# Embedding gathers spread over the first items' loop, the row table filled in a small and a large pass, and both norms of the first layer taken from one set of statistics

## The reference, cut to what matters

```python
h = jnp.take(W.T, x, axis=0)          # x: (16, 256) ids below 12564; W: (256, 50257) -> 4096 rows of 256 floats
t = _layernorm(h)                      # no gain, no shift
for l in range(6):                     # "attention" over the 16 sequences
    n = layernorm(t, gamma[l], beta[l])
    q, k, v = split(n @ w_qkv[l]); q = softmax(q, axis=1); k = softmax(k, axis=2)
    ctx = einsum('bic,bjc->bij', k, v)
    t = einsum('bic,bij->bjc', q, ctx) @ w_out[l] + b_out[l] + t
h = h + t
# then top-2 of 8 experts (SwiGLU) and a shared expert on layernorm(h), added to h
```

## Time and profile before

| what | value |
|---|---|
| median of 3 runs | 1470.19 us (1468.88 to 1470.64) |
| the profiled execution's own time | 1476.68 us |
| its span, first to last instruction | 1474.9 us |
| mean granted TensorE clock | 0.946 |
| PE / DVE / ACT / POOL busy | 87% / 71% / 56% / 65% of the span |
| DMA traffic | 157.13 MB, mean 107 GB/s |

### The profile page before, as it was taken

The page is one execution under the profiler, slowest core; times in us unless marked ns, Lnnn a source line. Parts: engine busy times, 40 slices in busy tenths (PEclk is TensorE's granted clock), DMA queues, the critical chain, the costliest instruction groups (busy, mean ns, idle before and its releaser), DMA issues. The chain is left out here.

```text
span 1474.9 us, 37041 instructions
## 1 busy us (share of the span) xinstructions
PE 1277.8 (87%) x10992; PEld 1053.6 (71%) x10993; DVE 1043.0 (71%) x2675; ACT 831.4 (56%) x2286; POOL 960.0 (65%) x958
## 2 busy tenths in 40 slices
PE   4400499999999999999999999879989999999996
PEld 3400388888888888888888888645557888788884
DVE  3245789998998899899889999756564444444442
ACT  1230388778778877787787777765632322222221
POOL 0057789889889888988898889558640333333333
PEclk8755799999999999999999999979999999999998
DMA  9993264543463355346332546554433434444440
GB/s 320 380 319 118 47 127 102 138 87 69 102 133 64 64 131 108 64 89 142 70 65 58 116 87 107 97 84 127 128 125 102 67 54 58 70 57 58 63 60 8
DMA packets 354415, 157.13 MB, mean 107 GB/s; under 512 B 283953, under 2 KB 338737, under 8 KB 354353
## 3 DMA queue, kind: packets, MB, share of 16 engines
q1 hardware_dynamic: 321090, 117.99, 35.8%
q0 software_dynamic: 20064, 25.32, 9.3%
q10 hardware_dynamic: 13200, 13.11, 2.5%
HBM read 44.50 MB, written 42.64 MB: 59 GB/s over the span
## 5 line engine op out<-in xcount | busy, mean ns | idle before, releaser
L731 PE MATMUL bank<-hT,Wc 128*128 128x256 f16 x2304 | 285.8, 274 | 88.0 <-DMA hT<-hhl 76.0
L731 PEld LDWEIGHTS bank<-hT,Wc 128*128 128x128 f16 x2304 | 226.7, 98 | 115.9 <-issue 88.5
L691 POOL DMA_INDIRECT out_rows<-h0b,payin x78 | 121.5, 1557 | 235.4 <-DVE h0b L1471 182.8
L828 PE MATMUL bank<-xTg,Wall 128*128 128x256 f16 x1872 | 211.1, 273 | 0.0
L828 PEld LDWEIGHTS bank<-xTg,Wall 128*128 x1872 | 183.2, 98 | 21.4
L1096 ACT ACTIVATE silu<-bank 128x512 f32<-128x512 f32 x110 | 65.6, 596 | 215.0 <-PE bank L828 177.0
L596 POOL TENSOR_TENSOR h0b<-h0b,rows 128x512 f32<-128x512 f32 x96 | 121.9, 1269 | 98.0 <-issue 52.6
L1399 DVE SCALAR_TENSOR_TENSOR gT<-bank,silu 128x512 f32<-128x512 f32 x110 | 76.0, 691 | 130.2 <-ACT silu L1096 124.3
L731 PE MATMUL bank<-Wc,MT 128*128 128x256 f16 x1152 | 143.3, 275 | 9.8 <-DVE MT L1262 9.8
L731 PE MATMUL bank<-khl,eqT 128*128 128x256 f16 x1152 | 142.4, 274 | 6.0 <-DVE khl L1274 0.3
L731 PE MATMUL bank<-Wc,hT 128*128 128x256 f16 x1152 | 142.0, 273 | 0.0
(11 more groups left out here) (150 smaller groups left out, 2585.8 us busy)
## 6 DMA issues: line engine op xcount, KB each, us to landing
Wall<-in_L_tok_W SPq DMA_DIRECT2D x25, 512.0 KB, 7.8
emb_rows<-Wall ACTq DMA_DIRECT2D x25, 512.0 KB, 11.7
Wall<-in_L_ffn_ew SPq DMA_DIRECT2D x24, 512.0 KB
Wc<-Wn SPq DMA_DIRECT2D x48, 128.0 KB
Wst<-in_L_attn_w_qkv SPq DMA_DIRECT2D x12, 384.0 KB
h_rows<-Wall SPq DMA_DIRECT2D x4, 1024.0 KB, 4.4
X<-h_rows POOLq DMA_DIRECT2D x8, 512.0 KB, 6.6
out_rows<-X SPq DMA_DIRECT2D x8, 512.0 KB
```

Source lines behind the costliest of these rows:

```text
L691: pool.indirect_dma_start(out=out_rows, out_offset=bass.IndirectOffsetOnAxis(ap=got(j % PAYS, w, 0, i32), axis=0), in_=yout[j % 2][:, w, : ...
L731: last = mm(to, lhs(a, k, o), moving, start=(i == 0 and k == 0), stop=(i == 2 and k == 1))
L828: last = mm(to, cols(a, e, 2 * k + w, (2 * half + c) * P, P), moving, start=(n_ == 0), stop=(n_ == 5))
```

## The change

It has five parts.
1. The table is split in two DRAM tensors. `emb_near` has 2560 rows (one step) and is filled and gathered from in a loop of passes; `emb_last` has 10240 rows (`VLAST` = 4 steps) and is filled once. With these ids there is one pass, then the four steps. A gather from either tensor skips the rows whose index is out of its bounds. A block of 512 rows of `emb_last` is first filled with zeros (`s_fill`).
2. POOL issues 32 gathers from `emb_near` as soon as the first step has landed, then moves the indices on by 2560 (an index that was already served is moved out of reach). The gathers from `emb_last` are issued item by item, two for each: items 0 and 1 ahead of the loop, item t+7 inside iteration t.
3. For layer 0 there are no `first_stats`, `first_root` and `first_norm`. The statistics are taken of `G`; if v is the variance, POOL computes the inverse roots of v+eps and of v(1+eps)+eps^2, and the two norms follow from these. DVE in `norm` makes two small products (`eratio`), the doubly normed row, and from it X with b_out added, which POOL did before. For items 0 to 15 ACT makes the high half of h (`hhl`) and POOL the fp32 form and the low half.
4. The first layer's weights are loaded ahead of steps 2 to 5 of the table, split between the chunks of step 2, and installed before the table's end. The first twelve iterations are written out (`HEAD`), and the splitting of layer 1's weights runs in iterations 3 to 10.
5. `G` is stored to `h0_rows` in eight pieces inside the loop. The experts' slices are converted in layers 1 to 3, one in every iteration, so the first eight iterations of each of these layers have both a CUT and a slice.

```diff
-            n = stretches(pool)
+            n = passes(pool)
             with pool.Fori(0, n) as q:
                 for j in range(VBUF):
-                    pool.wait_ge(s_wst[j], (q + 1) * (STRETCH * 16))
+                    pool.wait_ge(s_wst[j], (q + 2) * 16)
                 pool.sem_inc(s_passed, 1)
+                for t in range(NT):
+                    gather(t, emb_near, s_gath[t % 4])
                 for g in range(4):
-                    gather(g)
-                for g in range(4):
-                    pool.wait_ge(s_gath[g], (q + 1) * 128)
+                    pool.wait_ge(s_gath[g], (q + 1) * (16 * NT // 4))
                 pool.sem_inc(s_passed, 1)
-
-                pool.tensor_scalar(idx[:, :], idx[:, :], -VROWS, None, ALU.add).then_inc(s_reuse, 1)
+                pool.tensor_scalar(far[:, :], idx[:, :], VSTEP, FAR, ALU.is_lt, ALU.mult).then_inc(s_far, 1)
+                pool.wait_ge(s_far, q * 2 + 1)
+                pool.sem_inc(s_passed, 1)
+                pool.tensor_tensor(idx[:, :], idx[:, :], far[:, :], ALU.add).then_inc(s_far, 1)
+                pool.wait_ge(s_far, q * 2 + 2)
+                pool.sem_inc(s_passed, 1)
+                pool.tensor_scalar(idx[:, :], idx[:, :], -VSTEP, None, ALU.add).then_inc(s_reuse, 1)
...
+            for j in range(VBUF):
+                pool.wait_ge(s_wst[j], (n + VLAST + 1) * 16)
+            pool.sem_inc(s_passed, 1)
+
+            def gather_item(i):
+
+                if i >= 4:
+                    pool.wait_ge(s_item[i % 4], 16 * TB * (i // 4))
+                for t in range(TB * i, TB * (i + 1)):
+                    gather(t, emb_last, s_item[i % 4])
...
+                if early(t + 4) and t >= 0:
+                    pool.wait_ge(s_hh, t + 5)
+                    low_half(t + 4, p)
+                if early(u):
+                    pool.wait_ge(s_rows, 48)
+                    pool.wait_ge(s_xb, u + 1)
+                    pool.tensor_tensor(xn[:, :, :], xn[:, :, :], row(0), ALU.mult).then_inc(s_hg, 1)
+                    pool.wait_ge(s_hg, u + 1)
+                    if u >= 1:
+                        pool.wait_ge(s_h, u)
+                    pool.tensor_tensor(hf[:, :, :], xn[:, :, :], row(1), ALU.add).then_inc(s_hf, 1)
+                    if t + 7 < NB:
+                        gather_item(t + 7)
+                    if t < -1:
+                        pool.wait_ge(s_hh, u + 1)
+                        low_half(u, 1 - p)
...
+                if early(w):
+                    pool.wait_ge(s_amv, w + 1)
+                    if w >= 2:
+                        pool.wait_ge(s_xb, w - 1)
+                    pool.tensor_scalar(evar[p][:, TB:], amv[p][:, :, 1], EPS, None, ALU.add)
+                    pool.tensor_scalar(evar[p][:, 0:TB], amv[p][:, :, 1], 1.0 + EPS, EPS * EPS, ALU.mult, ALU.add).then_inc(s_avar, 1)
+                    pool.wait_ge(s_avar, w + 1)
+                    pool.tensor_tensor(erstd[p][:, :], evar[p][:, :], mhalf[:, 0:2 * TB], ALU.pow).then_inc(s_arstd, 1)
...
+            act.dma_start(emb_last[VROWS - 2 * VCH:VROWS - VCH, :].rearrange("(v p) d -> p v d", p=P), h0b[:, 0, :, :]).then_inc(s_fill, 16)
...
+                    chunk(step, j, emb_last, VROWS - VCH if f_ == VLAST - 1 and j == VBUF - 1 else r0)
+                    if f_ == 0:
+                        for n_ in range(2 * j, min(2 * j + 2, WSL)):
+                            cut(n_, 0, n_)
...
+                i = t + 5 if isinstance(t, int) and t < -1 else t + 4
+                if early(i) and t != -1:
+                    act.wait_ge(s_hf, i + 1)
+                    if i >= 2:
+                        act.wait_ge(s_hT[i % 2], landed(i - 2))
+                    A(hhl[i % 2][:, 0, :, :], hf[:, :, :], ACT.Copy).then_inc(s_hh, 1)
...
+                if early(w):
+                    for k in range(TB):
+                        last = V.scalar_tensor_tensor(eratio[:, k:k + 1], evar[p][:, k:k + 1], erstd[p][:, k:k + 1],
+                                                      erstd[p][:, TB + k:TB + k + 1], ALU.mult, ALU.mult)
+                    last.then_inc(s_quot, 1)
+                    for k in range(TB):
+                        last = V.tensor_scalar(xn[:, k, :], G[:, w * TB + k, :], amv[p][:, k, 0:1], erstd[p][:, k:k + 1],
+                                               ALU.subtract, ALU.mult)
+                    last.then_inc(s_xn, 1)
...
+                    for k in range(TB):
+                        last = V.scalar_tensor_tensor(X[:, w * TB + k, :], xn[:, k, :], eratio[:, k:k + 1], rows[:, 0, 2, :],
+                                                      ALU.mult, ALU.add)
+                    last.then_inc(s_xb, 1)
+                    return
...
+                    if l == 0 and i in (1, 2, 3, 4, 5, 6, 7, 9):
+                        store_h0((i - 1) if i < 8 else 7)
+                    if l == 0 and i in (8, 10, 12):
+                        load_expert(0, (i - 8) // 2)
+                    if l == 1 and i < 1:
+                        load_expert(1, i + 2)
+                    if l in (1, 2) and 2 <= i < 11:
+                        load_expert(3 * l - 1 + (i - 2) // 3, (i - 2) % 3)
```

More of the change, by code:

```diff
@@ L299, in tower @@
         AHEAD = 6
-        PLAIN, CUT, EXPERT, LAST = range(4)
+        PLAIN, CUT, LAST = range(3)
+        HEAD, FIRST_CUT = 12, 3
         def item_loop(eng, one, lead, other=True, between={}, unroll=0):
@@ L311, in hook @@
                     between[t]()
-            quarter = NB // 4
-            for t in range(-lead, 2):
-                one(t, t % 2, CUT if other and t >= 0 else PLAIN, None)
+            half, quarter = NB // 2, NB // 4
+            for t in range(-lead, HEAD if other else 2):
+                one(t, t % 2, CUT if FIRST_CUT <= t < FIRST_CUT + WSL else PLAIN, None)
                 hook(t)
@@ L320, in item_loop @@
             else:
-                with eng.Fori(1, quarter) as h:
-                    pair(h, CUT)
[L323 to L329, removed]
+                with eng.Fori(HEAD // 2, half) as h:
+                    pair(h, PLAIN)
+                with eng.Fori(1, 4) as l:
+                    with eng.Fori(0, quarter) as b:
+                        pair(eng.snap(l * half + b), CUT, eng.snap((l - 1) * half + b))
+                    with eng.Fori(quarter, half) as b:
+                        pair(eng.snap(l * half + b), PLAIN, eng.snap((l - 1) * half + b))
+                with eng.Fori(4 * half, 4 * half + quarter) as h:
+                    pair(h, CUT)
                 start = (ITEMS - AHEAD - XPER) // 2
-                with eng.Fori((ITEMS - NB) // 2, start) as h:
+                with eng.Fori(4 * half + quarter, start) as h:
                     pair(h, PLAIN)
@@ L594, in one @@
                     pool.sem_inc(s_passed, 1)
-                    row = lambda r: rows[:, bass.ds(layer(u) % 2, 1), r, :].broadcast_to([P, TB, D])
                     pool.tensor_tensor(xn[:, :, :], xn[:, :, :], row(0), ALU.mult).then_inc(s_hg, 1)
@@ L1171, in staged_last @@
                 return lastf[:, bass.ds((n - (XALL - XPER)) * XCH, XCH)]
[L1173 removed]
+            m = passes(dve)
             def chunk(step, j):
                 dve.wait_ge(s_wtr[j], step + 1)
[L1177 to L1178 removed]
+                dve.wait_ge(s_wst[j], (step + 1) * 16)
                 V.tensor_copy(VR[j][:, 2:4, :].rearrange("p a b -> p (a b)"), pb[2 * (j % 4) + 1][:, :]).then_inc(s_wcp[j], 1)
[L1181 to L1182 removed]
@@ L1221, in _ @@
             dve.wait_ge(s_route, 2)
-            for g in range(4):
-                first_stats(g)
-            first_norm(0)
             def stats_of(g):
@@ L1300, in one @@
                     last.then_inc(s_amv, 1)
-            item_loop(dve, one, AHEAD, between={**{2 * g - 7: partial(first_norm, g) for g in range(1, 4)},
-                                                **{ITEMS - 6 + g: partial(stats_of, g) for g in range(6)}})
+            item_loop(dve, one, AHEAD, between={ITEMS - 6 + g: partial(stats_of, g) for g in range(6)})
             add(ITEMS - 1)
```

220 lines of the change are left out of this document (110 added, 110 removed).

## The result

| | before | changed |
|---|---|---|
| median of the runs | 1470.19 us (5 runs, 1467.74 to 1470.72) | 1460.3 us (5 runs, 1459.68 to 1464.22) |
| profiled execution, its span | 1476.68, 1474.9 us | 1461.73, 1460.0 us |
| item 0 on POOL, PE's first product | 136.24, 146.25 us | 99.51, 109.60 us |
| item 16 on POOL | 274.53 us | 264.77 us |

A forecast was written before the change was run, and what follows sets the result against it. PE paces the loop after a 146 us start where it is not the limit; item 16 27.3 us earlier, plus 1.5 for later layers, gives -25.8 from 1470.2: 1444 us, range 1427 to 1458.

The forecast's parts named there:

- The table and the near pass: Start: table ends at 89.1 us instead of 82.15; near pass ends at 84.5, hidden with 4.6 us to spare.
- A: The table's end in the changed kernel: 82.15 + 6.0 - 1.1 + 2 = 89.1 us.
- a skipped row moves nothing: Near gathers: a skipped row costs no transfer; the rival, that it costs as a moved one, 8.4 us later, chance 0.06.
- The rival of the late near pass: Start, on POOL: near pass ends late and everything behind waits; at 2.5 us a gather 1476 us; chance 0.06.
- The first item: Start of layer 0: POOL begins item 0 at A + 9.6, PE starts at A + 19.4 = 108.5 us instead of 146.25.
- The ramp: Items 1 to 4, engines taking turns: 10.0 us an item, 12.5 for item 4, reaching A + 52.1.
- the overlap: Layer 0 from iteration 0: POOL's low half and a CUT lie beside DVE's norm, adding nothing to the cycle.
- the cycle of 8.9 us: Layer 0 loop: 2.1 + 2.5 + 2.7 + 1.5 = 8.8, with handing over 8.9; items 6 to 14 at this pace.
- The gathers in the loop: POOL, layer 0: 1.34 us each with issue; rival of 1.81 us beside VectorE gives 1457 us, chance 0.11.
- Later layers: First eight iterations of layers 1 to 3: 0.06 us each, 1.5 us for 24; rival 0.5 each, 1455 us, chance 0.07.
- Iterations that lose a slice gain nothing: Later layers: iterations without their former slice get no faster, as PE paces them.

The follow-up runs named there:

- low_half_8_columns: Changed kernel, but POOL's low half of h covers only 8 columns for items 2 to 15; 1478.85 us, kernel before beside it 1477.19 us.
- norm_beside_gathers_alone: Changed kernel with POOL reordered in layer 0: gathers before the norm wait, low half and CUT moved off the norm; 1468.87 us, kernel before 1477.19.

## Why the prediction was wrong, step by step

**The table and the near pass** were right in the result's session: A was 90.35 for 89.1, near pass hidden, a skipped row moves nothing. The rival of the late near pass named the right culprit and the wrong mechanism: in the late sessions the near pass does not itself end late (its index work is at 83.5 us in `low_half_8_columns`), it holds up the table under which it was to be hidden. I had priced what the near pass moves under the table, 0.84 MB, and nothing for the transfers beside it.

**The first item** was right: A + 9.2 for 9.6, PE at 109.6 for 108.5. **The ramp** was 10.3 us an item for 10.0, item 4 13.3 for 12.5.

**The step that failed** is the overlap: "From iteration 0 the low half lies after the root and so beside the norm, and so does a CUT", from which the cycle of 8.9 us follows. Beside the norm they are not free; they stop it. Items 6 to 14 took 94.8 us for 80.1, 14.7 more, and item 5 1.1 more.

The rows split these 15.8 us. The block itself, the pair's time above 0.35 us, is 8.1. In items 8, 10 and 12 the norm starts 1.2 us after its root, 3.6 together; in `low_half_8_columns`, where the block is nearly gone, it is 0.2 to 0.3, so I take this to follow from the block too. In item 6 it is 2.2 us, and there it is 2.5 in `low_half_8_columns`: this is not the block, and why DVE comes late there no run shows. The rest, 1.9, is the path itself: from item to root POOL took 6.9 us, and with 2.0 of norm and 0.2 of handing over that is 9.1 a round for 8.9. With 0.8 at item 0, 1.7 in items 1 to 4 and -0.7 in items 15 and 16 the 15.8 make the 17.6 us by which item 16 was missed (264.77 for 247.2). Where only gathers lie beside the norm, as in `norm_beside_gathers_alone`, rounds are 8.6 to 9.1, two of 9.7 apart; but there the gathers have left POOL's path and the low half and CUT have joined it, so it is another sum than the one forecast. The sign was in the rows already: in the earlier trace rows DVE's norm took 1.08 us beside POOL's CUT, and 0.73 with POOL idle in the earlier trace rows. I had read that row for its price of a CUT only.

The Trainium skill, "SBUF — State Buffer", section "SBUF: two separate sides", states the rule for this place too: the port pair is an exclusive lock for a whole instruction, and among the VectorE operations that want it are those with two inputs in SBUF, against a GpSimd operation that reads SBUF, and those in a two-port mode. The traces agree: the ratios and the norm (SBUF only) stood still beside CUT and low half, operations with a bank among their inputs did not, and nor did the norm beside gathers. I had applied the section to the gathers alone, where the price turned out near nothing.

**The gathers in the loop** at 1.34 us were right: 1.0 to 1.15 busy and 0.3 of issue.

**Later layers** cost nothing in sum where I had 1.5 us: the gain is 9.8 us at item 16, 8.5 at item 61, 10.1 at item 78 and 10.0 at item 95. Up to item 61 the forecast was about right. Over the eight iterations of a layer that have both CUT and slice, a round on POOL takes 8.46 us in the mean, where the same iterations took 8.34 to 8.37 before, so 0.1 each where I took 0.06. "Iterations that lose a slice gain nothing" holds as well: in the last eight of layer 4 it is 8.08 for 8.11. What gives the time back is the eight CUT iterations of layer 4, which have no slice in either kernel: 8.18 for 8.34. No run shows why, so that the sum came to nothing is luck.

## What to carry to other kernels

Work "beside" a norm is hidden only if the two engines may work at the same time: before costing a move at nothing, find a row where the same pair of operations already overlaps, and compare it with the same operation alone. When a wait of one engine ends as another's unrelated operation ends, look at what both touch. A stage put under a transfer-bound stage must be priced for what its issue does to those transfers, not for its bytes, and a gain of 1% from it should be timed in more than one session.

## What the runs showed of the hardware

- A VectorE operation on SBUF operands waited for GpSimd's elementwise operations inside its own recorded time: two ratios of one column took 0.35 us alone and up to 2.02 beside a low half; with an operand in PSUM, 0.69 us both ways. Beside gathers the ratios took 0.34 us.
- An indirect gather whose rows are all out of bounds, but for a possible id 0, still makes its packets (1536 for 32 gathers, with 0.02 MB for 0.90). With near gathers in the program, the DMAs moved 123 to 156 GB/s from 56 to 88 us in three sessions, where it was 357 to 382 in the other three. Why in some sessions and not in others, no run tells: the changed kernel was early in two and late in two, with the same program, and of the two sessions on one chip (the chip numbered 4) one was early and one late. Nor do they tell whether it is issue or packets.
- The kernel before, whose gathers lie behind its table, had its first item at 136.2 and 135.8 us in an early and a late session.
